# A two-layer network on one core: the second layer's attention products on half the array's rows, from a compact state

## The reference, cut to what matters

```python
q = jax.nn.relu((x @ Wq.T + bq).reshape(B, N, H, HD))      # H = 16, HD = 32
k = jax.nn.relu((x @ Wk.T + bk).reshape(B, N, H, HD))
v = (x @ Wv.T + bv).reshape(B, N, H, HD)
kv = jnp.einsum('bnhd,bnhp->bhdp', k, v)                   # one 32x32 block a head
k_sum = k.sum(axis=1)
denom = jnp.maximum(jnp.einsum('bnhd,bhd->bnh', q, k_sum), 1e-6)[..., None]
out = (jnp.einsum('bnhd,bhdp->bnhp', q, kv) / denom).reshape(B, N, C)
y = out + x                                                # then a layernorm
```

## Time and profile before

| | us |
|---|---|
| median of 3 runs | 2073.2 |
| lowest, highest | 2072.14, 2074.89 |
| the profiled execution | 2074.62 |
| its span, first to last instruction | 2072.8 |

### The profile page before, as it was taken

One profiled execution on the slowest core, in us unless ns is written; L12 is line 12 of the kernel. 1 busy time (PEld: TensorE's weight loads), 2 busy tenths in 40 slices (PEclk: granted clock), 3 DMA queues, 4 the chain that ended last, 5 costly groups with the idle time before them and its releaser, 6 DMA issues.

```text
span 2072.8 us, 27462 instructions
## 1 busy us (share of the span) xinstructions
PE 2056.4 (99%) x9243; PEld 1644.1 (79%) x9243; DVE 1525.8 (74%) x3004; ACT 1094.5 (53%) x1843; POOL 835.0 (40%) x842
## 2 busy tenths in 40 slices
PE   9999999999999999999999999999999999999998
PEld 6887888444688888888888888888888888888887
DVE  5998875666687777777777875677777676777776
ACT  3555555323455555555555555755555555555553
POOL 1001110344545444454445453144444444444444
PEclk9999999999999999999999999999999999999999
DMA  5756663886533333333333333422222222222211
GB/s 191 260 203 221 200 218 120 277 270 208 173 125 110 102 121 104 114 120 102 122 113 112 108 127 102 153 72 72 72 72 84 88 83 91 83 72 71 72 42 41
DMA packets 179892, 263.73 MB, mean 127 GB/s; under 512 B 20392, under 2 KB 110760, under 8 KB 177192
## 3 DMA queue, kind: packets, MB, share of 16 engines
q1 hardware_dynamic: 166488, 238.18, 34.6%
q10 hardware_dynamic: 13264, 23.79, 3.2%
HBM read 161.14 MB, written 100.79 MB: 126 GB/s over the span
## 4 chain that ended last, share of the span: by engine, by line
PE 88%; DVE 5%; ACT 2%; DMA 2%; issue 2%; POOL 1%; SPq 0%; ACTq 0%; POOLq 0%
PE bank L102 22%; PE bank L104 22%; PE bank L103 22%; PE bank L1521 7%; PE bank L2069 3%; PE bank L910 3%; PE bank L931 3%; PE bank L928 3%; PE bank L1477 2%; DMA bv_row<-in_L_attn_bv 1%; DVE e_w_lo L1896 0%; DVE d_x L1374 0%; DVE d_xq L1345 0%; DVE d_stats L1376 0%; DVE d_q_max L1337 0%
## 5 line engine op out<-in xcount | busy, mean ns | idle before, releaser
L102 PE MATMUL bank<-e_ring,e_w_hi 128*128 128x512 f32 x512 | 200.7, 392 | 0.0
L103 PE MATMUL bank<-e_ring,e_w_hi 128*128 128x512 f32 x512 | 199.3, 389 | 0.0
L104 PE MATMUL bank<-e_ring,e_w_lo 128*128 128x512 f32 x512 | 199.2, 389 | 0.0
L1521 PE MATMUL bank<-d_kh,d_nat 128*128 128x512 f32 x768 | 191.2, 398 | 0.0
L1789 POOL TENSOR_TENSOR e_x<-e_x,e_beta 128x512 f32<-128x512 f32 x64 | 91.4, 1446 | 217.0 <-ACT e_y L1832 217.0
L1143 POOL TENSOR_TENSOR rstd<-d_var_eps,neg_half 128x1 f32<-128x1 f32 x64 | 35.6, 556 | 339.1 <-DVE d_var_eps L1385 339.1
L1843 ACT ACTIVATE e_kr<-bank 128x512 f32<-128x512 f32 x64 | 38.0, 593 | 243.9 <-PE bank L104 243.9
L1521 PEld LDWEIGHTS bank<-d_kh,d_nat 128*128 128x128 f32 x768 | 139.7, 188 | 26.9
L1914 DVE TENSOR_TENSOR e_ring<-e_mixed,e_ring 128x512 fp32r<-128x512 f32 x128 | 93.5, 731 | 88.0 <-ACT e_ring L1807 87.9
L1771 POOL TENSOR_TENSOR e_x<-e_x,e_ff 128x512 f32<-128x512 f32 x64 | 83.3, 1302 | 174.8 <-DVE e_ff L1980 174.8
L1390 DVE TENSOR_TENSOR d_nat<-d_xn,d_nat 128x512 fp32r<-128x512 f32 x64 | 85.9, 1344 | 78.2 <-ACT d_nat L1250 78.2
(11 more groups left out here) (223 smaller groups left out, 6286.8 us busy)
## 6 DMA issues: line engine op xcount, KB each, us to landing
scr_v<-b_vt SPq DMA_DIRECT2D x64, 256.0 KB, 2.7
scr_z<-b_zt SPq DMA_DIRECT2D x64, 256.0 KB, 2.1
c_z<-scr_z SPq DMA_DIRECT2D x64, 256.0 KB, 4.3
scr_y<-c_y ACTq DMA_DIRECT2D x64, 256.0 KB, 3.9
d_x<-in_L_attn_x SPq DMA_DIRECT2D x64, 256.0 KB, 3.5
d_v<-scr_v SPq DMA_DIRECT2D x32, 512.0 KB, 5.2
scr_x<-d_x SPq DMA_DIRECT2D x64, 256.0 KB, 2.2
scr_xnt<-d_xt SPq DMA_DIRECT2D x32, 512.0 KB, 4.1
```

The lines of the kernel that those rows point to most:

```text
L102: eng.matmul(out, lhs[hi], rhs[hi], start=first, stop=False, skip_group_check=onto)
L103: eng.matmul(out, lhs[hi], rhs[lo], start=False, stop=False, skip_group_check=onto)
L104: return eng.matmul(out, lhs[lo], rhs[hi], start=False, stop=last, skip_group_check=onto)
L1521: mm = pe.matmul(BG[c][:, :], s[:, i, cols], r[:, j, :], start=M % NTB == 0 and i == j, stop=M % NTB == NTB - 1 and i == 1, skip_group_che ...
```

## The change: the state in halves, two products for each

The state keeps 66 columns instead of 132 for each group of 128 channels. The rows 0 to 63 hold the two heads of the lower half in columns 0 to 63, the rows 64 to 127 those of the upper half in the same columns 0 to 63, and the two columns behind them the key sums of the two heads. Each product becomes two, c = 0 and c = 1, on rows 0 to 63 and 64 to 127 of queries and state: 64 rows, 128 stationary columns, 66 moving ones. Half c of all four groups goes into bank CB[c]. VectorE's operations read 4 pieces of 66 columns a bank instead of 2 of 132, and the multiplication for half c writes the blocks of 64 channels c, c + 2, c + 4, c + 6 of `att`. The bytes that the tile `kv` gives up are skipped, so that the tiles behind it keep their addresses.

```diff
--- before.py
+++ after.py
@@ -1395,7 +1395,7 @@
             dve.wait_ge(keep["set"], 3)
             for j in range(HP):
                 rows = slice(j * HD, (j + 1) * HD)
-                nc.vector.tensor_copy(keep["kv"][rows, b, :, P + j:P + j + 1], BA[rows, 0:KT].unsqueeze(2))\
+                nc.vector.tensor_copy(keep["kv"][rows, b, :, P // 2 + j % 2:P // 2 + j % 2 + 1], BA[rows, 0:KT].unsqueeze(2))\
                   .then_inc(kv_done, 1)
             if b:
                 dve.wait_ge(kv_done, HP * ((KT + 1) * b))
@@ -1408,7 +1408,7 @@
                 rows = slice(j * HD, (j + 1) * HD)
                 for t in range(KT):
                     own = slice(t * P + j * HD, t * P + (j + 1) * HD)
-                    nc.vector.scalar_tensor_tensor(keep["kv"][rows, b, t, j * HD:(j + 1) * HD],
+                    nc.vector.scalar_tensor_tensor(keep["kv"][rows, b, t, j % 2 * HD:(j % 2 + 1) * HD],
                                                    keep["bv_row"][rows, own], ksum[rows, t:t + 1], BA[rows, own],
                                                    ALU.mult, ALU.add).then_inc(kv_done, 1)
 
@@ -1633,7 +1633,7 @@
     KT, D, GT, GN, NG, NGB, NCB, B = sh.KT, sh.D, sh.GT, sh.GN, sh.NG, sh.NGB, sh.NCB, sh.B
     HD = D // HEADS
     HP = P // HD
-    KVC = P + HP
+    HALF, KVC = P // 2, P // 2 + HP // 2
     small = areas["tables"].tile
 
     def over(tile, name, shape, dt=F32, skip=0):
@@ -1664,8 +1664,8 @@
     y = [over(f"d_x{i}", f"e_y{i}", [P, D]) for i in range(GT)]
     gamma = over("d_bk", "e_gamma", [P, D])
     beta = areas["rest"].tile("e_beta", [P, D])
-    den = small("e_den", [P, 2, 2, HP])
-    rden = small("e_rden", [P, 2, 2, HP])
+    den = small("e_den", [P, 2, KT, HP // 2])
+    rden = small("e_rden", [P, 2, KT, HP // 2])
     stats = small("e_stats", [P, 6])
     moments = [small(f"e_moments{i}", [P, 2]) for i in range(2)]
     var_eps = small("e_var_eps", [P, 1])
@@ -1985,8 +1985,8 @@
             if n:
                 dve.wait_ge(rden_done, n)
             for c in range(2):
-                sums = CB[c][:, 0:2 * KVC].rearrange("p (a x) -> p a x", a=2)
-                nc.vector.tensor_scalar(den[:, c, :, :], sums[:, :, P:KVC], DENOM_EPS, None, ALU.max)\
+                sums = CB[c][:, 0:KT * KVC].rearrange("p (a x) -> p a x", a=KT)
+                nc.vector.tensor_scalar(den[:, c, :, :], sums[:, :, HALF:KVC], DENOM_EPS, None, ALU.max)\
                   .then_inc(den_done, 1)
             dve.wait_ge(den_done, 2 * (n + 1))
             nc.vector.reciprocal(rden[:, :, :, :].rearrange("p c a j -> p (c a j)"),
@@ -1995,11 +1995,11 @@
             if n >= 2:
                 dve.wait_ge(sum_done, n - 1)
             for c in range(2):
-                sums = CB[c][:, 0:2 * KVC].rearrange("p (a x) -> p a x", a=2)[:, :, 0:P]
+                sums = CB[c][:, 0:KT * KVC].rearrange("p (a x) -> p a x", a=KT)[:, :, 0:HALF]
                 nc.vector.tensor_tensor(
-                    att[t % 2][:, c * 2 * P:(c + 1) * 2 * P].rearrange("p (a j d) -> p a j d", a=2, j=HP),
-                    sums.rearrange("p a (j d) -> p a j d", j=HP),
-                    rden[:, c, :, :].unsqueeze(3).broadcast_to([P, 2, HP, HD]), ALU.mult).then_inc(c_done, 1)
+                    att[t % 2][:, :].rearrange("p (a c j d) -> p c a j d", a=KT, c=2, j=HP // 2)[:, c, :, :, :],
+                    sums.rearrange("p a (j d) -> p a j d", j=HP // 2),
+                    rden[:, c, :, :].unsqueeze(3).broadcast_to([P, KT, HP // 2, HD]), ALU.mult).then_inc(c_done, 1)
 
         def tile_stats(g, t):
             n = g * GT + t
@@ -2066,8 +2066,10 @@
             if n:
                 pe.wait_ge(c_done, 2 * n)
             for a in range(KT):
-                mm = pe.matmul(CB[a // 2][:, a % 2 * KVC:(a % 2 + 1) * KVC], qt[:, a, t * P:(t + 1) * P],
-                               keep["kv"][:, b, a, :], start=True, stop=True)
+                for c in range(2):
+                    rows = slice(c * HALF, (c + 1) * HALF)
+                    mm = pe.matmul(CB[c][:, a * KVC:(a + 1) * KVC], qt[rows, a, t * P:(t + 1) * P],
+                                   keep["kv"][rows, b, a, :], start=True, stop=True)
             mm.then_inc(c_full, 1)
 
         def body(g):
@@ -2172,7 +2174,7 @@
     }
     mem = Stretch(nc, SBUF_AT)
     keep = {
-        "kv": mem.tile("kv", [P, B, KT, P + 4]),
+        "kv": mem.tile("kv", [P, B, KT, P // 2 + 2]),
         "shift1": mem.tile("shift1", [P, NT]),
         "rstd1": mem.tile("rstd1", [P, NT]),
         "cols": mem.tile("cols", [P, 8 * KT]),
@@ -2183,6 +2185,7 @@
     keep["rstd0"] = mem.tile("rstd0", [P, NT])
     keep["bv_row"] = mem.tile("bv_row", [P, D])
     keep["consts"] = mem.tile("consts", [P, P + 16])
+    mem.at += 4 * B * KT * (P // 2 + 2)
     after_ident = mem.at
     keep["into_t"] = mem.tile("into_t", [P, NO, NS])
     keep["toep_t"] = mem.tile("toep_t", [P, NO, CHUNK])
```

## The result

The changed kernel takes 2096.3 us (median of 4 runs, 2095.8 to 2098.7), the one before 2073.4 (4 runs, 2072.1 to 2074.9): 1.0114 of the time, 95% interval 1.0102 to 1.0126. It is slower by 22.9 us. The forecast was 2102, in a range of 2080 to 2155. Of the runs further down, one of same_half (2815.4 us, granted clock 0.714) and one of extra_both (2327.1 us, 0.85) fell into a slower state of the chip and are left out of their medians.

The account below looks back on a forecast made before the run. TensorE was taken to bound the kernel. Per tile 0.09 going in, 1.00 loads, 0.055 last pass and 0.20 coming back make 1.35 us against 0.90; +28.8 us over 64 tiles gives 2102 us, range 2080 to 2155.

Parts of the forecast that it names:

- The bound: Second layer: TensorE sets the span; at line 2069 load alone 0.1116 us, streaming 0.111, and the change halves only streaming.
- The loads overlap: Split products: 64-row loads keep 0.1116 us, but loads of different halves run beside each other; forecast's chance 0.45.
- rival 1: Split products: halves load one after the other, shape changes cost as forecast; +1.23 us a tile, 2152 us; chance 0.26.
- rival 2: Split products: halves load one after the other, shape change costs nothing; +0.89 us a tile, 2130 us; chance 0.09.
- Rival 3: Split products: loads overlap or cost half in sequence, shape change free; 0.89 us against 0.90, 2073 us; chance 0.15.
- rival 4: Split products: half-price loads that also overlap, shape change free, streaming bounds; -0.46 us a tile, 2044 us; chance 0.05.
- The steps: Split products: a tile's 16 loads take 1 + 8 steps, 9 x 0.1116 = 1.00 us, the first exposed.
- A2: Split products, order A1 A2 B1 B2: first half's second load, assumed to follow that half's first pass.
- B1: Split products, order A1 A2 B1 B2: second half's first load, assumed to run beside A2.
- The change of shape: Around each tile's half-height products: 0.09 us going in, 0.20 coming back, taken from line 639.
- The sum: A tile's products and shape change: 1.35 us against 0.90, +0.45 us; 64 tiles give +28.8 us.
- What cost nothing: VectorE's new patterns, the state's writers and waits for the banks' release: 0 us each.

Follow-up runs that it names:

- same_half: The changed kernel with both half products of each group reading rows 0 to 63, channels 64 to 127 left out; 2153.1 us, 1.0391 of the time before.
- extra_both: The kernel before plus two half-height products per tile, rows 0 to 63 into the first bank, 64 to 127 into the second; 2111.8 us, 1.0178.
- full_height_twice: The changed kernel with each of its eight products per tile on all 128 rows, 66 moving columns; 2132.2 us, 1.0287 of the time before.
- extra_half: The kernel before plus one product per tile on rows 0 to 63 alone, 66 moving columns, result unread; 2108.9 us, 1.0172.
- halves_apart: The changed kernel with the product loops swapped: all four products on rows 0 to 63 first, then four on rows 64 to 127; 2126.9 us, 1.0262.
- two_stretches: The changed kernel with each tile's half-height passes split into two stretches, in 60 of 64 tiles; 2117.6 us, 1.0212 of the time before.
- two_tiles: The changed kernel with two tiles' products made together after the second's matmuls, key sums left out; 2125.4 us, 1.0255 of the time before.
- extra_full: The kernel before plus one product per tile on all 128 rows, 128 stationary and 66 moving columns, result unread; 2087.2 us, 1.0066.
- extra_narrow: The kernel before plus one product per tile on all 128 rows with 8 stationary columns, result unread; 2099.4 us, 1.0125.

## Why the prediction was right, and what was off

**The bound.** Right. The product's time was its loads', and TensorE was the path. Halving the moving columns gained nothing: full_height_twice streams 66 columns and still goes at 0.11 us a pass.

**The loads overlap.** Right, but with no row behind it, and taken narrowly (0.45, rival 1 at 0.26). On the rows alone it was a guess that came true: nothing in the trace of the kernel before could have decided it. same_half is rival 1 made real, 2153.1 us for the forecast's 2152, and full_height_twice is rival 2, 2132 for 2130. Rival 3 falls with extra_half, rival 4 with the pace of 0.11 us a pair.

**The steps.** Here a term was mis-sized. I took 9 steps, since I let A2 pair with B1 in the written order. The trace has the first two loads at once, and 16 loads are 8 steps. halves_apart shows the reason: the other half's load is pulled ahead of loads that still wait. Its pass goes with it: pass records also start in pairs 7 ns apart, and the second of a pair can't be A2's, whose load starts 0.11 us later. One step less is -0.11 us a tile, -7 us.

**The change of shape.** Right in kind, place and size. The stretches in the chain give it by themselves. Passes of half height over n steps took

| | steps | us in the chain | 0.145 + n x 0.1116 |
|---|---|---|---|
| extra_half | 2 | 0.36 | 0.37 |
| two_stretches | 4 | 0.59 | 0.59 |
| the changed kernel | 8 | 1.04 | 1.04 |
| same_half, two_tiles | 16 | 1.93 | 1.93 |

and 0.145 is the forecast's 0.09 + 0.055, going in and the last pass. Coming back is 0.20, as forecast. The price of one excursion beyond its load steps is thus 0.145 + 0.20 = 0.345 us; extra_half against extra_full gives 0.34 and two_stretches 0.34 to 0.36. What share of the 0.20 is the load that nothing hides, and what share a drain, no run parts. The Trainium skill's rule that a change of the tiling mode drains the engine (TensorEngine Tiling (Array Packing), Key Properties) agrees with the 0.35 us of idle time before the first half-height load.

**What was left out.** The matmuls behind the sixteen passes take 0.03 us more a tile, +2 us, and full_height_twice shows the same without a change of shape. What causes it stays open.

**The sum.** 28.8 - 7.1 + 1.9 = 23.6 us by the corrected terms, 22.9 measured. Without the two errors, of opposite sign, the forecast would have been 2097 instead of 2102. The range held the result in its lower quarter. It was wide for the rivals' sake, not for the forecast's own.

**What cost nothing** did: VectorE's patterns, the state's writers, the banks' release. No wait for VectorE stands before line 2071.

No run beat the kernel before. Pairing tiles saves every second excursion, but even the expected 2084 us, without the key sums and never reached, is above 2073: eight load steps a tile remain in either form, since a half-height load on its own takes as long as a full one and there are twice as many.

## What to carry to other kernels

Before a product is cut to fewer rows of the array, ask what sets its pace: take a product of the same stationary shape with hardly any moving columns from the same trace (line 1528 here), and if it goes as fast, cutting the columns gains nothing. Splitting the rows leaves the loads' total as it was at best, when the halves alternate in the written order, and each return trip between shapes costs about 0.35 us here, so such products belong in long stretches or not into a stream of full-height work. Putting them into long stretches has its own price where another engine takes the results in order.

## What the hardware showed that was not expected

- The load of another half was pulled past three waiting loads of the first, and not past more, though its half was free from the start (halves_apart, 12.5 steps against 8, alike in all 64 tiles). Its passes went ahead with it, so passes of different halves don't keep the written order among themselves. One kernel is the only evidence of the depth, and whether it counts loads or all instructions is not shown.
- Loads of the same rows do overlap a running matmul at full height: in the earlier trace rows, where all is at full height, matmuls are busy 300.00 us and loads 252.18 of the same 300. Line 2069 says so without the recorded ends: its load alone takes 0.11 us, its streaming alone 0.11, and a pass with both 0.1125. The Trainium skill's page TensorE: Matmul & The Clock Gate (The mechanism) says that a load overlaps a running matmul only when the row groups differ; the trace doesn't bear that out. The same section also lets a load for the background weight buffer go ahead of a running matmul, and with that the trace agrees.
- A product of 8 stationary columns on all rows paid 0.43 us for the next matmul, as the half-height ones did (extra_narrow). The forecast had assumed it; the trace of the kernel before had it for line 639 alone.
